# Adding expert rows to the residual in DRAM: one accumulating scatter in place of a store, a load of pairs and a sum

## The reference, cut to what matters

```
xn  = layernorm(x)
s   = latent_attention(xn)
x2  = xn + attention(rmsnorm(xn)) @ Wo.T            # 16 heads, causal
n   = rmsnorm(x2) * w_ln2
for each token: the 2 of 8 experts with the largest logits n @ Wr.T, gates = softmax of these two logits
moe = sum over the two experts e of  gate_e * (Wd[e] @ (silu(Wg[e] @ n) * (Wu[e] @ n)))   # inner width 512
out = x + s * silu(x2 + moe)
```

## Time and profile before

| | |
|---|---|
| median of 3 runs | 976.75 us (970.0 to 980.24) |
| profiled execution | 980.88 us |
| its span, first to last instruction | 979.1 us |
| mean granted TensorE clock | 0.945 |
| busy, share of the span: TensorE (PE) | 86% |
| VectorE (DVE) | 68% |
| ScalarE (ACT) | 51% |
| GpSimd (POOL) | 27% |
| DMA: read from and written to HBM | 57.35 MB, 12.71 MB |
| scatters of expert rows | 46, mean 1.249 us of GpSimd each |

### The profile page before, as it was taken

The page is one execution under the profiler, slowest core; times in us unless marked ns, Lnnn a source line. Parts: engine busy times, 40 slices in busy tenths (PEclk is TensorE's granted clock), DMA queues, the critical chain, the costliest instruction groups (busy, mean ns, idle before and its releaser), DMA issues.

```text
span 979.1 us, 20037 instructions
## 1 busy us (share of the span) xinstructions
PE 838.6 (86%) x6688; PEld 748.5 (76%) x6688; DVE 662.8 (68%) x2345; ACT 502.0 (51%) x1090; POOL 268.6 (27%) x286
## 2 busy tenths in 40 slices
PE   5879999999989999998998999976169999999940
PEld 3858988977887887797797797764169999999940
DVE  4877668667667766857866866833257777777726
ACT  3436465365356456355445536533046777777721
POOL 5520400320230221131041032010404454545333
PEclk9988999999999999999999999977589999999985
DMA  8000000000000000000000000030245656588434
GB/s 272 1 1 2 13 2 12 13 2 2 22 0 2 12 11 2 12 11 2 11 12 1 12 12 1 2 141 22 41 137 188 241 191 240 191 302 302 166 119 171
DMA packets 33535, 70.88 MB, mean 72 GB/s; under 512 B 10786, under 2 KB 24994, under 8 KB 30498
## 3 DMA queue, kind: packets, MB, share of 16 engines
q1 hardware_dynamic: 26866, 57.39, 16.8%
q0 software_dynamic: 5440, 12.13, 4.0%
q10 hardware_dynamic: 1152, 0.49, 0.3%
HBM read 57.35 MB, written 12.71 MB: 72 GB/s over the span
## 4 chain that ended last, share of the span: by engine, by line
PE 67%; DVE 14%; issue 9%; DMA 3%; SPq 3%; ACT 2%; POOL 1%; DVEq 0%; ACTq 0%; POOLq 0%
PE ps L575 55%; PE ps L668 5%; PE ps L705 3%; DVE ps L1399 2%; DVE ps L1402 2%; DVE negm L1402 1%; PE ps L601 1%; SPq L422 1%; DMA ln<-in_w_ln 1%; DVE negm L1399 1%; PE ps L902 1%; DMA yl<-expert_rows 1%; PE ps L610 1%; SPq L437 1%; DMA raw<-in_w_experts 1%
## 5 line engine op out<-in xcount | busy, mean ns | idle before, releaser
L1094 ACT ACTIVATE ex<-ps 128x384 f32<-128x384 f32 x256 | 125.6, 496 | 137.9 <-PE ps L575 126.6
L575 PE MATMUL ps<-qt,kt 128*128 128x256 f32 (+1 forms) x768 | 164.9, 325 | 9.5 <-issue 6.0
L503 POOL TENSOR_TENSOR tok<-tok,swp 128x256 f32<-128x256 f32 x128 | 97.2, 760 | 219.2 <-DVE swp L1354 218.2
L1399 DVE CUSTOM_DVE_ANT_0 ps<-ps,mask 128x128 f32<-128x128 f32 x256 | 76.4, 298 | 77.7 <-PE ps L575 45.3
L575 PEld LDWEIGHTS ps<-qt,kt 128*128 128x128 f32 x768 | 109.2, 193 | 18.6 <-issue 10.4
L1402 DVE CUSTOM_DVE_ANT_0 ps<-ps,mask 128x256 f32<-128x256 f32 x256 | 119.3, 466 | 0.0
L1233 DVE TENSOR_TENSOR wel<-raw,weh 128x768 fp32r<-128x768 f32 x92 | 88.2, 958 | 37.8 <-ACT weh L962 36.4
L575 PE MATMUL ps<-wh,xth 128*128 128x320 f32 (+2 forms) x352 | 95.7, 354 | 6.3 <-DVE wl L1233 3.7
L1350 DVE TENSOR_TENSOR tok<-ps,cos_t 128x320 f32<-128x320 f32 x128 | 62.8, 491 | 52.6 <-PE ps L575 46.8
L546 POOL DMA_INDIRECT expert_rows<-yo,slot_of x46 | 57.5, 1249 | 128.9 <-ACT yo L1195 121.9
L575 PE MATMUL ps<-xeh,weh 128*128 128x256 f32 x368 | 78.5, 295 | 11.7 <-issue 11.7
(11 more groups left out here) (167 smaller groups left out, 1958.4 us busy)
## 6 DMA issues: line engine op xcount, KB each, us to landing
raw<-in_w_experts SPq DMA_DIRECT2D x23, 1536.0 KB
yl<-expert_rows SPq DMA_DIRECT2D x4, 1024.0 KB, 5.4
mla_branch<-s_b SPq DMA_DIRECT2D x8, 256.0 KB, 2.1
x_normalised<-otk SPq DMA_DIRECT2D x8, 256.0 KB, 2.2
xr<-in_x SPq DMA_DIRECT2D x1, 2048.0 KB
s_tok<-mla_branch SPq DMA_DIRECT2D x1, 2048.0 KB
out<-xr SPq DMA_DIRECT2D x4, 512.0 KB, 2.9
w_cols_raw<-in_w_cols SPq DMA_DIRECT2D x1, 1792.0 KB, 15.9
```

The source lines that it names most:

```text
L503: nc.gpsimd.tensor_tensor(t, t, swp[:, n % 2, :, :], ALU.add).then_inc(tokd, 1)
L575: return nc.tensor.matmul(o, a, m, start=start, stop=stop, skip_group_check=True, **k)
L1094: nc.scalar.activation(ex[:, h % (2 * G), :], ps[4 + h % 2][:, P:4 * P], ACT.Exp, scale=scale).then_inc(ex_, 1)
L1399: nc.vector.tensor_tensor_reduce(out=o[:, 0:P], in0=o[:, 0:P], in1=mask2[:, 1, :], scale=-1.0, scalar=-2.0 * BIG, op0=ALU.add, op1=ALU.min ...
```

## The change

Both results of a token now go to the same row, on top of `x2`.
- SP also stores `x2` (unscaled, from `xn`) into the first 2048 rows of `expert_rows`, one store of 256 KB for each sequence (`keep_x2`, semaphore `x2k`). In the loop it stands before `store_x2`; for the last sequence it stands behind it.
- The records name the token itself as the destination, and the two DVE additions that step the ids become one.
- The scatters add to DRAM (`compute_op=ALU.add`). All count on one semaphore. The first block's scatters wait for all of `x2k`; those of block b wait until all scatters of the blocks before have landed. Within one block no destination occurs twice. `keep_y` of block b waits, as before, for block b - 2.
- The pair loads, the GpSimd sums and the DVE additions of the tail are gone. SP loads `x2` plus both results into `x3` in five chunks of 4, 4, 4, 2 and 2 tiles of 128 tokens, with a buffer for each and no wait between. silu, multiplication, addition and store go by the same five chunks.

```diff
-TC = 512
-NC = T // TC
+ENDS = (slice(0, 4), slice(4, 8), slice(8, 12), slice(12, 14), slice(14, 16))
+NC = len(ENDS)
-YROWS = 2 * T + SLOTS
+YROWS = T + SLOTS
...
+            x3_v = ys[0:T, :].rearrange("(t p) e -> p t e", p=P)
+
+            def keep_x2(r):
+                sp.wait_ge(x2d, r + 1)
+                sp.dma_start(x3_v[:, bass.ds(2 * r, 2), :], xn[:, bass.ds(2 * r, 2), :]).then_inc(x2k, 16)
...
             with sp.Fori(1, last) as b:
                 row1(b)
+                keep_x2(b - 1)
                 store_x2(b - 1)
...
             row1(last)
+            keep_x2(last - 1)
             store_x2(last - 1)
...
             store_x2(last)
+            keep_x2(last)
...
-            sp.wait_ge(ysd[0], 16 * BT * ((NB + 1) // 2))
-            sp.wait_ge(ysd[1], 16 * BT * (NB // 2))
-            y_v = ys[0:2 * T, :].rearrange("(t p k) e -> p t (k e)", p=P, k=2)
-            for j in range(NC):
-                if j > 1:
-                    sp.wait_ge(x3d, j - 1)
-                sp.dma_start(yl[:, j % 2, :, :, :].rearrange("p t k e -> p t (k e)"),
-                             y_v[:, 4 * j:4 * j + 4, :]).then_inc(yld[j], 16)
+            sp.wait_ge(ysd, 16 * BT * NB)
+            for t, loaded in zip(ENDS, x3d):
+                sp.dma_start(x3[:, t, :], x3_v[:, t, :]).then_inc(loaded, 16)
             o_v = out.rearrange("(t p) e -> p t e", p=P)
-            for j in range(NC):
+            for j, t in enumerate(ENDS):
                 sp.wait_ge(fin, j + 1)
-                sp.dma_start(o_v[:, 4 * j:4 * j + 4, :], xr[:, 4 * j:4 * j + 4, :]).then_inc(s_out, 16)
+                sp.dma_start(o_v[:, t, :], xr[:, t, :]).then_inc(s_out, 16)
...
             def scatter(blk):
                 pool.wait_ge(yod, blk + 1)
+                if blk == 0:
+                    pool.wait_ge(x2k, 16 * B)
+                else:
+                    pool.wait_ge(ysd, 16 * BT * blk)
                 for j in range(BT):
                     nc.gpsimd.indirect_dma_start(ys[:, :], bass.IndirectOffsetOnAxis(mt_b[:, blk, j, 1:2], 0),
-                                                 yo[:, blk % 2, j, :], None).then_inc(ysd[blk % 2], 16)
+                                                 yo[:, blk % 2, j, :], None, compute_op=ALU.add).then_inc(ysd, 16)
...
-            for j in range(NC):
-                pool.wait_ge(yld[j], 16)
-                if j > 1:
-                    pool.wait_ge(x3d, j - 1)
-                nc.gpsimd.tensor_tensor(ysum[:, j % 2, :, :], yl[:, j % 2, :, 0, :], yl[:, j % 2, :, 1, :],
-                                        ALU.add).then_inc(ysumd, 1)
...
             def keep_y(blk):
                 act.wait_ge(dd, IT * (blk + 1))
                 if blk >= 2:
-                    act.wait_ge(ysd[blk % 2], 16 * BT * (blk // 2))
+                    act.wait_ge(ysd, 16 * BT * (blk - 1))
...
             def ffn_silu(j):
-                act.wait_ge(x3d, j + 1)
+                act.wait_ge(x3d[j], 16)
                 if j >= 2:
                     act.wait_ge(mud, j - 1)
-                nc.scalar.activation(gl[:, j % 2, :, :], xn[:, 4 * j:4 * j + 4, :], ACT.Silu).then_inc(gld, 1)
+                t = ENDS[j]
+                nc.scalar.activation(gl[:, j % 2, 0:t.stop - t.start, :], x3[:, t, :], ACT.Silu).then_inc(gld, 1)
...
-                nc.vector.tensor_scalar(step[:, :, 0], step[:, :, 0], 2.0 * P, None, ALU.add)
-                nc.vector.tensor_scalar(step[:, :, 1], step[:, :, 1], 4.0 * P, None, ALU.add).then_inc(gst, 1)
+                nc.vector.tensor_scalar(step[:, :, :], step[:, :, :], 2.0 * P, None, ALU.add).then_inc(gst, 1)
...
-            def result(j):
-                t = slice(4 * j, 4 * j + 4)
-                dve.wait_ge(ysumd, j + 1)
-                nc.vector.tensor_tensor(xn[:, t, :], xn[:, t, :], ysum[:, j % 2, :, :], ALU.add).then_inc(x3d, 1)
...
             for j in range(NC):
-                result(j)
-                if j >= 1:
-                    combine(j - 1)
-            combine(NC - 1)
+                combine(j)
```

More of the change, by code:

```diff
@@ L218, in build @@
         gl = sb("gl", [P, 2, 4, E], F32, moe)
-        yl = sb("yl", [P, 2, 4, 2, E], F32, moe)
-        ysum = sb("ysum", [P, 2, 4, E], F32, moe)
+        x3 = sb("x3", [P, TT, E], F32, moe)
         moe.close()
@@ L335, in build @@
         yod = sem("y_kept")
-        ysd = [sem("y_scattered_even"), sem("y_scattered_odd")]
+        ysd = sem("y_added")
+        x2k = sem("x2_stored_for_sums")
         xrd = sem("x_again")
-        yld = [sem(f"y_rows_loaded_{i}") for i in range(NC)]
-        ysumd = sem("y_summed")
-        x3d = sem("moe_added")
+        x3d = [sem(f"x3_loaded_{i}") for i in range(NC)]
         gld = sem("ffn_silu")
@@ L1670, in combine @@
                 dve.wait_ge(gld, j + 1)
-                nc.vector.tensor_tensor(s_tok[:, t, :], s_tok[:, t, :], gl[:, j % 2, :, :], ALU.mult).then_inc(mud, 1)
+                nc.vector.tensor_tensor(s_tok[:, t, :], s_tok[:, t, :], gl[:, j % 2, 0:t.stop - t.start, :], ALU.mult).then_inc(mud, 1)
                 dve.wait_ge(mud, j + 1)
@@ L1732, in laid_out @@
     ids[..., 0] = i[:, None, None] + P * np.arange(2)[None, :, None]
-    ids[..., 1] = 2 * ids[..., 0] + np.arange(2)[None, None, :]
+    ids[..., 1] = ids[..., 0]
     j = np.arange(NDYN)
@@ L1739, in laid_out @@
     slots = np.zeros((SLOTS, 4), np.uint32)
-    slots[:, 1] = 2 * T + np.arange(SLOTS)
+    slots[:, 1] = T + np.arange(SLOTS)
     consts = dict(cosines=cosines, sines=sines, ident=np.eye(P), mask=mask, mask_t=mask.T, seen_t=np.where(i[:, None] > i[None, :], 0.0, BOUND),
```

## The result

Over 12 runs each on one chip the changed kernel takes 963.32 us (960.77 to 969.11) and the one before 974.47 (970.0 to 980.24): ratio 0.9889, 95% interval 0.9867 to 0.9911, so 10.8 us less (the two medians are 11.15 apart). The profiled execution of the changed kernel took 961.99 us for a span of 960.2.

A forecast was written before the change was run, and what follows sets the result against it. TensorE bounds the blocks, but the unhidden tail of load, GpSimd sum, DVE and store is where the change works. Span 979.1 - 14.6 (tail) + 3.0 (adding scatters) = 967.5, so median 965.2 against 976.75; range 958.5 to 975.

The forecast's parts named there:

- T0: End of the block stage: all scatters landed and SP issues the first load of sums; forecast 3.0 us later.
- the sum: Whole span: 979.1 - 14.6 for the tail + 3.0 for later scatter landing = 967.5 us.
- The reading of the block stage: Stage of 23 blocks, 722 to 945 us: TensorE sets the pace, 9.77 us a block; nobody waits for a scatter.
- The tail: From all scatters landed to the span's end: 17.75 us instead of 32.36, 14.6 less.
- the multiply of 3.37 us: Tail on DVE: one multiply overlapping a GpSimd sum took 3.37 us, others 1.22; without sums it can't recur.
- my high end: Adding scatters: fetch a round trip and each issue doubled to 1.92 us; pair 7.4, scatters all landed 6.8 later.
- X: Time from a block's first scatter issue to the landing of both: 3.66 us plain, 5.5 forecast for adding scatters.
- "Between blocks it hides: in 9.77 us even 7.4 leaves 2.4": Block stage: an adding pair of even 7.4 us fits the 9.77 us block period, so it costs nothing there.
- a sign of being wrong: Block stage: scatters starting late in its middle would show the forecast wrong.
- Rival 3: Block stage: the scatter chain becomes the bound once a pair passes 9.77 us; slower, about 1025 at 12; chance 0.13.
- "Gathers run three blocks ahead": GpSimd queue: the next gather stands behind the waiting scatter, but gathers have three blocks' lead; no cost counted.
- x2 stores, chunk issues on SP, slot steps: Eight 256 KB stores, five tail load issues of about 0.37 us, one DVE id addition fewer: all counted as nothing.

The follow-up runs named there:

- the second: The second profile of the changed kernel, from running it unaltered on another chip against the kernel before: 964.4 us, ratio 0.9876.
- the tail alone: Changed kernel's tail and x2 stores, with plain scatters to their own rows and no ordered wait, against the kernel before: 967.03 us, ratio 0.9857.
- the run with few weights: Changed kernel with weight loads of blocks 2 to 22 cut to an eighth of their columns, against the kernel before: 957.25 us, ratio 0.9803.
- Five buffers: Changed kernel with five row buffers instead of four, so gathers are issued one block earlier, against the kernel before: 964.39 us, ratio 0.9873.
- The ordered wait alone: Kernel before plus a wait of each block's plain scatters for those of the block before, against the kernel before: 981.57 us, ratio 1.0006.

## Why the prediction was right, point by point

- **What was luck.** T0's delay and the block stage together cost 5.7 us in the profile (6.8 in the second) where the sum has 3.0, and 1.9 (0.7) of it was given back up to block 1, where the slot lists went faster, which is not the change's doing. Counted by the ratios, against the tail alone, the cost is 1.9 to 3.1 us, with intervals as wide.
- **The reading of the block stage**: "TensorE waits for nothing but a few hundred ns of issue" overlooks 8.19 us at block 2, at 731.33, inside the very stretch that was read. The change doesn't touch that wait, so the sum stands, but it hid a bigger lever than the gathers or the chunks: the run with earlier weights, which removes it, is 7.1 us below the changed kernel.
- **The tail**: forecast T0 + 17.75, measured T0 + 17.77. First chunk 4.2 forecast, 4.07 measured; DVE's start 5.35 against 5.22; DVE's end 15.15 against 15.15 (957.58). The row-size argument held, and the multiply of 3.37 us did not recur. The last store took 2.62, forecast 2.6. The fit of the Trainium skill (DMA: Bandwidth & Descriptors, Anatomy of one DMA), which is for DMAs issued by GpSimd, would have made the first chunk 3.2; the trace had 4.07, so the row was the better guide.
- **T0**: forecast 3.0 us later, measured 4.0 counted from the last block's results, and 1.9 to 3.1 by the ratios (0.9876 and 0.9889 against 0.9857 for the tail alone). The length of the pair was nearly right, 5.5 forecast and 5.75 measured, but for half wrong reasons. I had the issue unchanged at 0.96 and the landing 1.84 longer. Measured: the issue is 1.55, and the landing 0.91 longer. The errors, 1.2 one way and 0.9 the other, cancelled. Both surcharges of my high end, a fetch as a full round trip and twice the issue time, were too dear; 7.4 was not reached. The lag of the last pair was forecast at 1.2 and is 1.9 more than before, since block 21 took 6.49 from issue to landing and not 5.8. The estimate from the Trainium skill (Collectives: The Full Stack, The bandwidth ceiling), X of 4.7 by doubling only the data, was too low; and worked out again, that X gives a T0 1.4 us later, not 1.7.
- **"Between blocks it hides: in 9.77 us even 7.4 leaves 2.4"** was wrong as a step and right in its result. That X was measured at the end of the program, where the engines are idle. Beside weight loads a pair took 9.0 to 11.3 us, the run with few weights shows why, and GpSimd waited at least 16 times. This met a sign of being wrong that I had named myself, scatters that start late in the middle of the block stage, and another failed too: issues of 1.55 to 2.2 us where I had 1.0. It was right in its result only so far as `keep_y` needs a scatter two blocks later, and never waited for one. What it cost came by the gathers, next but one.
- **Rival 3** (slower: the chain becomes the bound) came far closer than 0.13 suggests: the spacing was 9.91 where I put equality at 9.9. Still, the chain did not set the pace: TensorE's blocks took 9.86 in the same stretch, and the lag grew from 1.8 to 2.6 us only. My formula 733.97 + 23X took one X for all blocks; it came near for the blocks with loads only; behind them the lag was made up within one block.
- **"Gathers run three blocks ahead"** was wrong. The gather of block b + 3 stands behind the scatters of block b - 1, and these wait for their own chain. Its lead was enough in all but one block. There TensorE waited 1.1 us (1.9 in the second profile), and the stage lost 1.6 to 2.9 us, which the traces show and the medians can't. Five buffers won most of it back.
- **x2 stores, chunk issues on SP, slot steps**: counted at nothing. The ordered wait alone gave 1.0006, and the tail alone with the stores gave 14.0 of the forecast 14.6, with an interval of 3 us; no cost of theirs is seen.

## What to carry to other kernels

Price a moved transfer where it will run, not where it is easy to see: a landing time read beside idle DMA engines was 5.7 us, and beside the loads of this kernel's main stage some 10. Where a wait is added to a queue, list everything behind it there, and count its lead in instructions of that queue and not in blocks. A chain of reading and writing at the end of a program pays in full; most of this gain was four sums, four additions and half of the loaded bytes less in a tail that no other work hides. When two profiles are compared, add up the stages one by one, down to those that the change does not touch: here one of them gave back 1.9 us that were not earned.

## What the runs showed of the hardware

An indirect scatter of 128 rows of 1 KB that adds took GpSimd 1.55 us to issue where a plain one took 0.96, made 96 packets more, and, as the second of a pair, landed 2.35 us after the end of its issue in place of 1.44, with the DMA engines otherwise idle. Beside weight loads of 1.5 MB a block, two of them took 9.0 to 11.3 us from first issue to landing; with loads of an eighth, about 6.2, an estimate from the median landing of 4.3. Plain ones in the same place made the next wait twice in 22, where they took 10.8 and 9.4 us.
